# Attention stage of a fused layer: a half's statistics and normalisation one slot earlier, and POOL's casts of the fourth slot behind its splits

## The chip, the cores and the metric

The kernel runs on one core of one Trainium2 chip. The metric is the device time of one execution in microseconds (us). Engines are named as the profile names them: PE (TensorE matmul), PEld (its weight loads), DVE (VectorE), ACT (ScalarE), POOL (GpSimd) and SP (SyncE, which here only issues DMAs).

## What is computed

The input x is (16, 1024, 256) in float32. Four residual stages follow each other: a linear recurrence over time (SSM), a small gated network (FFN), causal attention, and the FFN once more. Only attention is touched:

```python
x = x + attn(layernorm(x))
# attn: x_proj = x @ Wqkv + bqkv; q, k, v = x_proj split in three
#       each reshaped (not transposed) from (1024, 256) to (16 heads, 1024, 16)
#       softmax(causal(q @ k.T / 4)) @ v, back to (1024, 256), then @ Wproj + bproj
# layernorm: (x - mean) / sqrt(var + 1e-5) over the 256 channels, no weights
```

Because of the plain reshape, head h is made of tokens 64h to 64h+63. A sequence of 1024 tokens so splits into two independent **halves** of 512 tokens and 8 heads each, and each half into two **quads** of 4 heads.

## The kernel before, in words

`attention_phase` (L1148) handles batch element b (0 to 15) in four **slots** q = 0 to 3, written here as the first, second, third and fourth slot. Slot q does quad 4b+q, and each slot has 20 **steps** (STEPS). The program is a loop nest unrolled in Python: every engine has a function `slot(b, q)` that collects tasks with a due step (a number, whole or not) and sorts them by it (`in_order`, L1308). The number only sets the order of an engine's own queue. An engine runs its queue strictly in that order and waits at semaphores where it must.

What runs in a slot:

- **Second pass** (all 20 steps). PE forms scores of the slot's quad with the row maxima as an extra row of the operands (L1878), ACT exponentiates them (L1738), and PE multiplies by v (L1906). Three PSUM banks, `s2_ps`, go round.
- **First pass** (steps 0 to 13 for the next quad, units 4 to 17; steps 16 to 19 for the quad after that, units 0 to 3). PE forms the plain scores (L1856), two products a step (one for each group of rows), DVE takes their row maxima (L1637, L1640) in `maxima`. Three banks, `s1_ps`, go round, so PE may start product n only when DVE has finished the maxima of product n-3 (`first_wait`, L1840). DVE's maxima of steps 4 and 13 end with a reduction and a 32x32 transpose, whose result SP moves by DMA (`move_max`, L1354).
- **x events** (`x_events`, L1187): the work that shares the single bank `x_ps`. "heads", "turn" and "out" finish earlier results. "project" with j = 0, 1 transposes the normalised x of a half, j = 2 to 5 gives q and k (L1934), and j = 6, 7 gives v. An event that stands at step n is issued by PE in step n+1. For the half 2b+3 the events j = 0, 1 are at steps 13, 15 of the second slot, and j = 2 to 7 at steps 3, 7, 9, 11, 13, 15 of the third. For the half 2b+4, j = 0 to 5 are at steps 3, 7, 9, 11, 13, 15 of the fourth, and j = 6, 7 at steps 3 and 7 of the next element's first slot.
- **Splits**. ACT copies the result of a project event with j < 6 to one of three buffers `full` (L1748, L1750), and POOL's `split` (L1468) writes it as two float32r parts: a cast (L1478) and a subtraction (L1480). PE's project j = 2 waits for the splits of both j = 0 and j = 1 (L1927).
- **Casts**. `lay_out` (L1482) casts the q and k stacks of quad+3 from `staged`, which SP's `load_stack` (L1331) has filled with 12 DMAs, into `qs` and `ks` (L1492). Per slot there are two sides and two pieces of each side. A small POOL instruction (L1490) goes ahead of each side and takes its waits. PE first reads these stacks at step 16 of the next slot. SP's next `load_stack` waits for them (L1336).
- **Statistics and normalisation** of a half of x. SP loads x (`load_x`, L1317), DVE's `prepare` (L1598) computes mean and variance (four L1604, a memset at L1610, four L1612), and POOL's `rstds` (L1449) and `normalise` (L1455) compute the reciprocal deviation (L1451, L1453) and normalise in place in four pieces (L1458). PE's project j = 0 waits for this (`xn_ready`). The statistics' tile `moments` is single, so `prepare` waits at L1608 for the previous half's normalisation.

The due steps of this work are constants:

```python
LAY_OUT_AT, PREPARE_AT, PIECES = (6.3, 7.6, 10.2, 12.2), 6, 2
NORMALISE_AT = (14.4, 15.5, 16.5, 17.5)
```

A half is prepared in the first slot (half 2b+3) and in the third slot (half 2b+4). SP loads the x of half 2b+4 in the first slot of the same b (due step 4, L1387).

Of the kernel before, what the change touches and what calls it, by code (L numbers as in the profile page):

```python
# [1147 lines left out]
def attention_phase(nc, sem, identf, identb, x2, x3, wqkv, bqkv, wproj, bproj, qk_scratch, v_scratch):  # L1148
# [25 lines left out]
    STEPS = 2 * UNITS2  # L1174
    LEAD = 4
    EVACUATE_AT = (7, 1)
    LAY_OUT_AT, PREPARE_AT, PIECES = (6.3, 7.6, 10.2, 12.2), 6, 2
    NORMALISE_AT = (14.4, 15.5, 16.5, 17.5)

    X_PROLOGUE = 22  # L1180
    FULLS = 3
# [5 lines left out]
    def x_events(q, first, more, more2):  # L1187

        heads = [] if first and q == 0 else [(1, "heads", 0), (7 if q == 1 else 5, "heads", 1)]
        finish = [] if first else {0: [(9, "turn", 0), (11, "out", 0), (13, "turn", 1), (15, "out", 1)],  # L1190
                                   1: [(3, "turn", 2), (5, "turn", 3), (9, "out", 2), (11, "out", 3)]}.get(q, [])
        project = {0: [(3, 6), (7, 7)], 1: [(13, 0), (15, 1)], 2: [(3, 2), (7, 3), (9, 4), (11, 5), (13, 6), (15, 7)],
                   3: [(3, 0), (7, 1), (9, 2), (11, 3), (13, 4), (15, 5)]}[q] if (more2 if q == 3 else more) else []
        return sorted(heads + finish + [(s, "project", j) for s, j in project])

    def flags(b):
        if isinstance(b, int):
            return b == 0, b + 1 < NB, b + 2 < NB
        return False, True, True
# [4 lines left out]
    def x_base(b, q):  # L1204

        before = X_PROLOGUE + sum(x_count(i) for i in range(b)) if isinstance(b, int) else \
            x_count(None) * b + (X_PROLOGUE + x_count(0) - x_count(None))
        return before + sum(len(x_events(i, *flags(b))) for i in range(q))

    def projected(b, q):  # L1210

        return ((2 * b + 2, 0), (2 * b + 3, 1), (2 * b + 3, 1), (2 * b + 4, 0))[q]
# [9 lines left out]
    with ExitStack() as ctx:  # L1222
# [85 lines left out]
        def in_order(tasks):  # L1308

            for _, task in sorted(tasks, key=lambda x: x[0]):  # L1310
                task()

        with nc.Block() as block:
# [129 lines left out]
            def _(pool):  # L1443
# [5 lines left out]
                def rstds(hb):  # L1449
                    pool.wait_ge(moments_done, hb + 1)  # L1450
                    g.tensor_tensor(var_eps[:, :], moments[:, :, 1], eps[:, :], ALU.add).then_inc(eps_added, 1)  # L1451
                    pool.wait_ge(eps_added, hb + 1)
                    g.tensor_tensor(rstd[:, :], var_eps[:, :], minus_half[:, :], ALU.pow).then_inc(rstd_ready, 1)  # L1453

                def normalise(hb, s, t):  # L1455
                    if t == 0:
                        pool.wait_ge(rstd_ready, hb + 1)
                    last = g.tensor_scalar(xt[s][:, t, :], xt[s][:, t, :], moments[:, t, 0:1], rstd[:, t:t + 1],  # L1458
                                           ALU.subtract, ALU.mult)
                    if t == TT - 1:  # L1460
                        last.then_inc(xn_ready, 1)
# [6 lines left out]
                def split(hb, j, index):  # L1468

                    n = 6 * (hb - 3) + j  # L1470
                    k = n % len(full)
                    pool.wait_ge(x_free, index + 1 - X_PROLOGUE)
                    if j < KT:
                        high, low = xnT[0][:, j, :], xnT[1][:, j, :]
                    else:
                        high, low = parts[:, j - KT, 0, :], parts[:, j - KT, 1, :]
                        pool.wait_ge(side_stored[(j - KT) // 2], 32 * hb)
                    g.tensor_copy(high, full[k][:, :]).then_inc(rounded, 1)  # L1478
                    pool.wait_ge(rounded, n + 1)
                    g.tensor_tensor(low, full[k][:, :], high.bitcast(F32), ALU.subtract).then_inc(split_done, 1)  # L1480
# [56 lines left out]
                def v_bias(hb, e, index):  # L1537
                    if index < X_PROLOGUE:
                        pool.wait_ge(v_free, 2 * hb + e + 1)
                    else:  # L1540
                        pool.wait_ge(x_free, index + 1 - X_PROLOGUE)
                    g.tensor_tensor(v_tok[:, 2 * e:2 * e + 2, :], v_tok[:, 2 * e:2 * e + 2, :],
                                    bv_row[:, :].unsqueeze(1).to_broadcast([P, 2, D]), ALU.add).then_inc(v_ready, 1)

                def bias(b, r):
                    pool.wait_ge(res_loaded[r % 2], 32 * b + 16 * (r // 2 + 1))
                    g.tensor_tensor(x_res[r % 2][:, :, :], x_res[r % 2][:, :, :],  # L1547
                                    bp_row[:, :].unsqueeze(1).to_broadcast([P, 2, D]), ALU.add).then_inc(bias_added, 1)

                def slot(b, q):  # L1550
                    first, more, more2 = flags(b)
                    quad = 4 * b + q
                    tasks = []
                    for n, (at, kind, which) in enumerate(x_events(q, first, more, more2)):
                        if kind == "project" and which >= 6:
                            tasks += [(at + 3, lambda e=which - 6, n=n: v_bias(projected(b, q)[0], e, x_base(b, q) + n))]
                        elif kind == "project":
                            tasks += [(at + 2, lambda j=which, n=n: split(projected(b, q)[0], j, x_base(b, q) + n))]
                    if q < 2 and not first:
                        tasks += [(4, lambda r=r: bias(b - 1, r)) for r in (2 * q, 2 * q + 1)]  # L1560
                    if q in (0, 2) and (more, None, more2)[q]:
                        hb, s = ((2 * b + 3, 1), None, (2 * b + 4, 0))[q]
                        tasks += [(NORMALISE_AT[0], lambda: rstds(hb))]
                        tasks += [(NORMALISE_AT[t], lambda t=t: normalise(hb, s, t)) for t in range(TT)]
                    if more or q == 0:
                        for side in range(2):
                            for e in range(PIECES):
                                tasks += [(LAY_OUT_AT[PIECES * side + e],
                                           lambda side=side, e=e: lay_out(quad + 3, side, e, not first or q > 0))]
                    in_order(tasks)  # L1570

                def sequence(b):
                    for q in range(4):
                        slot(b, q)
# [20 lines left out]
            def _(dve):  # L1595
                v = nc.vector

                def prepare(hb, s, turn):  # L1598
                    if not isinstance(hb, int) or hb > 0:

                        dve.wait_ge(moments_done, hb)
                    dve.wait_ge(x_loaded[s], 16 * turn + 16)
                    for t in range(TT):
                        last = v.bn_stats(stats[:, t, :], xt[s][:, t, :])  # L1604
                    last.then_inc(stats_done, 1)
                    if not isinstance(hb, int) or hb > 0:

                        dve.wait_ge(xn_ready, hb)  # L1608
                    dve.wait_ge(stats_done, hb + 1)
                    v.memset(carrier[:, :], 0.0)  # L1610
                    for t in range(TT):
                        last = v.bn_aggr(moments[:, t, :], stats[:, t, :])  # L1612
                    last.then_inc(moments_done, 1)
# [56 lines left out]
                def slot(b, q):  # L1670
                    first, more, more2 = flags(b)
                    tasks = []
                    for step in range(STEPS):
                        unit = first_pass_at(q, step, more)
                        if unit is not None:
                            tasks += [(step, lambda unit=unit: maxima(4 * b + q + unit[0], unit[1]))]
                    for n, (at, kind, which) in enumerate(x_events(q, first, more, more2)):
                        if kind == "heads":
                            before = (q - 1) % 4
                            tasks += [(at + 1, lambda e=which, n=n: divide(4 * b + q - 1, before, e, x_base(b, q) + n))]  # L1680
                        elif kind == "out":
                            tasks += [(at + 1, lambda r=which, n=n: add(b - 1, r, x_base(b, q) + n))]
                    if q in (0, 2) and (more, None, more2)[q]:
                        tasks += [(PREPARE_AT, lambda: prepare(*((2 * b + 3, 1, b + 1), None, (2 * b + 4, 0, b + 2))[q]))]
                    in_order(tasks)

                def sequence(b):
# [387 lines left out]
```

## Time and profile before

| | |
|---|---|
| three timed runs | 4064.49, 4067.5 (median), 4070.07 us |
| the profiled execution's own time | 4071.99 us |
| its span in the profile | 4070.2 us, 78382 instructions |
| busy over the span | PE 3703.5 us (91%), DVE 2935.1 (72%), ACT 2248.6 (55%), POOL 1702.0 (42%) |
| mean granted TensorE clock | 0.966 of full |

All rows are of this one profiled execution. "Busy" is the time in which an engine had an instruction in execution; the ends of matmuls are modelled. Stage and slot borders below are the starts of ACT's first exponential (L1738) of a slot. In a timeline row the first number is the start in us from the span's start, the second the length, and the bracket, where there is one, the engine's idle time ahead of it and what ended it. Rows of several instructions ("x4") run from the first's start to the last's end.

### The profile page before, as it was taken

The page shows a single profiled execution, that of the slowest core. Times are in us where ns is not written, and L with a number is a line of the kernel's source. Part 1 is how long each engine was busy: PE and PEld are TensorE (multiplying, and loading weights), DVE is VectorE, ACT ScalarE, POOL GpSimd, SP SyncE. Part 2 cuts the span into 40 slices and gives each one's busy share as a digit, 9 for nine tenths or more (in the row PEclk, how much of TensorE's full clock was granted, in tenths as well). Part 3 has the DMA queues.
Part 4 walks back from the last instruction along what each step waited for, and adds up shares of the span by engine and source line. Part 5 has one row for each costly group of instructions (what it writes and reads, how often), then busy time and mean ns, then how long its engine had stood idle before and what let it go on. Part 6 is the DMA issues. An engine that isn't in the chain of part 4 may idle for free. (4 is left out here: it accounts for less than half of the span.)

```text
span 4070.2 us, 78382 instructions
## 1 busy us (share of the span) xinstructions
PE 3703.5 (91%) x26254; PEld 2383.8 (59%) x26254; DVE 2935.1 (72%) x9262; ACT 2248.6 (55%) x4454; POOL 1702.0 (42%) x2042
## 2 busy tenths in 40 slices
PE   4998799999479999999999999999999996999997
PEld 4887566666245555555555555555555553666674
DVE  6997466756467877887787778778877882466675
ACT  0100356665136666666666666666666663566664
POOL 2332024232625555555464555556455510142422
PEclk9999799999669999999999999999999997999999
DMA  1332111111566778677777767787777731021111
GB/s 54 98 103 91 55 47 63 63 45 39 108 113 101 117 103 127 103 115 121 115 115 106 123 112 114 107 121 111 112 124 109 112 43 58 32 63 63 60 45 42
DMA packets 701473, 361.36 MB, mean 89 GB/s; under 512 B 305072, under 2 KB 668080, under 8 KB 701104
## 3 DMA queue, kind: packets, MB, share of 16 engines
q1 hardware_dynamic: 701104, 356.65, 48.9%
q8 instruction: 206, 3.38, 0.4%
q14 instruction: 163, 1.34, 0.2%
HBM read 204.49 MB, written 150.99 MB: 87 GB/s over the span
## 5 line engine op out<-in xcount | busy, mean ns | idle before, releaser
L1738 ACT ACTIVATE att_probs<-att_s 128x512 f32<-128x512 f32 (+1 forms) x2560 | 1319.1, 557 | 754.5 <-PE att_s L1826 429.4
L1637 DVE CUSTOM_DVE_ANT_0 att_s<-att_s,att_above 128x384 f32<-128x384 f32 (+3 forms) x2048 | 957.4, 514 | 190.6 <-PE att_s L1856 190.5
L1878 PE MATMUL att_s<-att_qs,att_ks 49*128 49x512 f32 (+3 forms) x3072 | 916.6, 387 | 101.6 <-ACT att_probs L1738 29.0
L1856 PE MATMUL att_s<-att_ks,att_qs 48*128 48x512 f32 (+3 forms) x3072 | 961.2, 407 | 23.6 <-POOL att_ks L1492 13.5
L1640 DVE TENSOR_REDUCE att_maxima<-att_s 128x1 f32<-128x512 f32 x1024 | 668.4, 682 | 248.6 <-PE att_s L1856 243.3
L1878 PEld LDWEIGHTS att_s<-att_qs,att_ks 49*128 49x128 f32 x3072 | 459.5, 185 | 661.4 <-ACT att_probs L1738 435.9
L1906 PE MATMUL att_o_ps<-att_probs,att_vs 128*32 128x512 f32 (+3 forms) x6144 | 630.2, 497 | 0.5 <-ACT att_probs L1738 0.5
L1856 PEld LDWEIGHTS att_s<-att_ks,att_qs 48*128 48x128 f32 x3072 | 486.1, 188 | 41.1 <-issue 16.9
L1057 PE MATMUL ffn_h2p<-ffn_h,ffn_w 128*128 128x512 f32 x768 | 365.6, 599 | 3.0 <-ACT ffn_h L938 0.9
L1826 PE MATMUL att_s<-att_mask,att_places 64*128 64x64 bf16 (+1 forms) x3072 | 332.7, 205 | 0.0
L1547 POOL TENSOR_TENSOR att_x_res<-att_x_res,att_bp_row 128x512 f32<-128x512 f32 x64 | 81.3, 1283 | 527.6 <-DMA att_x_res<-x 527.1
L916 ACT ACTIVATE ffn_uv<-ffn_uvp 128x512 f32<-128x512 f32 x256 | 153.3, 599 | 251.4 <-PE ffn_uvp L1032 251.4
L1637 DVE DVE_READ_ACCUMULATOR2_ANT att_maxima<- 128x1 f32 x2048 | 288.6, 141 | 0.0
L1492 POOL CAST att_ks<-att_staged 113x1024 fp32r<-113x1024 f32 x128 | 253.5, 1993 | 0.0
L946 ACT ACTIVATE ffn_h<-ffn_turned,ffn_b 128x512 f32<-128x512 f32 x384 | 242.6, 684 | 17.4 <-PE ffn_turned L1048 15.5
L1492 POOL CAST att_qs<-att_staged 113x1024 fp32r<-113x1024 f32 x128 | 251.9, 1991 | 0.0
L938 ACT ACTIVATE ffn_h<-ffn_h2p,ffn_b 128x512 f32<-128x512 f32 x192 | 132.0, 687 | 198.2 <-PE ffn_h2p L1057 198.2
L1906 PEld LDWEIGHTS att_o_ps<-att_probs,att_vs 128*32 128x32 f32 x6144 | 134.1, 108 | 161.1 <-issue 121.6
L675 POOL TENSOR_TENSOR ffn_var_eps<-ffn_moments,ffn_eps 128x4 f32<-128x4 f32 x64 | 13.1, 204 | 500.8 <-DVE ffn_moments L760 500.8
L775 DVE TENSOR_TENSOR ffn_zT_lo<-ffn_zTp,ffn_zT_hi 128x512 fp32r<-128x512 f32 x128 | 87.8, 686 | 182.3 <-ACT ffn_zT_hi L908 182.3
L1934 PE MATMUL att_x_ps<-att_xnT,att_wqkv 128*128 128x512 f32 x714 | 200.7, 417 | 19.9 <-POOL att_xnT L1480 19.7
L1048 PEld LDWEIGHTS ffn_turned<-identf,ffn_uv 128*128 128x128 f32 x1536 | 175.5, 143 | 64.6 <-issue 43.5
(247 smaller groups left out, 6559.9 us busy)
## 6 DMA issues: line engine op xcount, KB each, us to landing
att_staged<-qk_scratch SPq DMA_DIRECT2D x768, 128.0 KB, 7.1
qk_scratch<-att_parts SPq DMA_DIRECT2D x128, 512.0 KB, 3.7
ffn_x<-x SPq DMA_DIRECT2D x64, 512.0 KB, 5.0
ssm_x<-in_L_attn_a_x_dram SPq DMA_DIRECT2D x32, 512.0 KB, 3.8
x<-ssm_y SPq DMA_DIRECT2D x32, 512.0 KB, 2.9
x<-ffn_y SPq DMA_DIRECT2D x32, 512.0 KB, 2.9
att_x<-x SPq DMA_DIRECT2D x32, 512.0 KB, 11.9
v_scratch<-att_v_tok SPq DMA_DIRECT2D x32, 512.0 KB, 3.5
```

What stands on the lines that cost most here:

```text
L946: last = a(h1[k][:, f, :], turned_ps[:, f, :], ACT.Gelu, bias=b1[:, f:f + 1])
L1048: last = pe.transpose(turned_ps[:, f, t * P:(t + 1) * P], of[:, t, f * P:(f + 1) * P], identf[:, :])
L1057: last = mm(h2_ps[:, :], w2[:, f, :], h1[k][:, f, :], start=(f == 0), stop=(f == KT - 1))
L1492: last = g.tensor_copy(stack[0:ROWS, :].rearrange("p (t c) -> p t c", c=HD)[:, e * n:(e + 1) * n, :], staged[side][0:ROWS, :, e * n:(e + 1 ...
L1637: last = v.tensor_tensor_reduce(scores, scores, above[:, CH - w:CH], 1.0, -3.0e38, ALU.add, ALU.max, to)
L1640: last = v.tensor_reduce(to, scores, AX.X, ALU.max)
L1738: a(probs[u % 2][2 * g + p][:, 0:n], bank[:, 0:n], ACT.Exp).then_inc(exp_done, 1)
L1826: last = mm(blocks[:, at, GROUP * half:GROUP * (half + 1)], places[rows, 2 * (1 - k) + half, :], mask[rows, 1 - k, 0:len(cols), :], start= ...
L1856: last = mm(bank[:, col:col + w], rows_of(qs[buf], g, KROWS, p, BT * blk, BT * (blk + 1)), rows_of(ks[buf], g, KROWS, p, t0, t1), start=k ...
L1878: last = mm(bank[:, col:col + w], rows_of(ks[buf], g, SHIFT + 1, p, BT * j, BT * (j + 1)), rows_of(qs[buf], g, SHIFT + 1, p, t0, t1), star ...
L1906: last = mm(o_ps[32 * i:32 * i + 32, HD * (t0 - first_t):HD * (t1 - first_t)], vs[s][:, NBLK * head + j, :], probs[u % 2][i][:, col:col + ...
L1934: last = mm(bank[:, :], wq[i][:, f, cols], xnT[k][:, f, :], start=(n == 0), stop=(n == KT * len(PARTS_R) - 1))
```

## The change

The first slot and the third slot prepared a half each. Now it is the first and the second: the half 2b+4 is measured by DVE (due step 6) and normalised by POOL (due steps 13.2, 14.7, 16.7, 18.7) in the second slot. The same due steps for POOL now hold in the first slot, too. In the fourth slot alone POOL's four casts get the due steps 10.2, 12.2, 14.2, 16.2, so that they stand behind the splits of j = 0 and 1 (due 5 and 9) and between those of j = 2 to 5 (due 11, 13, 15, 17). PE's, ACT's and SP's orders are untouched, and no instruction is added or taken away.

```diff
-    LAY_OUT_AT, PREPARE_AT, PIECES = (6.3, 7.6, 10.2, 12.2), 6, 2
-    NORMALISE_AT = (14.4, 15.5, 16.5, 17.5)
+    LAY_OUT_AT = [(6.3, 7.6, 10.2, 12.2)] * 3 + [(10.2, 12.2, 14.2, 16.2)]
+    PREPARE_AT, PIECES = 6, 2
+    NORMALISE_AT = (13.2, 14.7, 16.7, 18.7)
...
-                    if q in (0, 2) and (more, None, more2)[q]:
-                        hb, s = ((2 * b + 3, 1), None, (2 * b + 4, 0))[q]
+                    if q < 2 and (more, more2)[q]:
+                        hb, s = ((2 * b + 3, 1), (2 * b + 4, 0))[q]
                         tasks += [(NORMALISE_AT[0], lambda: rstds(hb))]
                         tasks += [(NORMALISE_AT[t], lambda t=t: normalise(hb, s, t)) for t in range(TT)]
...
-                                tasks += [(LAY_OUT_AT[PIECES * side + e],
+                                tasks += [(LAY_OUT_AT[q][PIECES * side + e],
...
-                    if q in (0, 2) and (more, None, more2)[q]:
-                        tasks += [(PREPARE_AT, lambda: prepare(*((2 * b + 3, 1, b + 1), None, (2 * b + 4, 0, b + 2))[q]))]
+                    if q < 2 and (more, more2)[q]:
+                        tasks += [(PREPARE_AT, lambda: prepare(*((2 * b + 3, 1, b + 1), (2 * b + 4, 0, b + 2))[q]))]
```

The half 2b+4 exists for b = 0 to 13 (`more2`), so both moves touch 14 elements.

## Rows read from the trace of the kernel before

**Rows 1.** Stretch, length; PE, PEld, DVE, ACT, POOL busy (instructions); PE's clock, DMA share, GB/s.

```profile
1170.90:3394.30 2223.40, 2114.30 (x18162) 1227.77 (x18161) 1751.74 (x5849) 1486.54 (x2981) 1150.50 (x1010) 0.99 0.72 108
```

**Rows 2.** PE's waits in the attention stage: total us, times, longest us.

```profile
PE att_s L1878 <- DVE att_maxima L1640: 28.6, 41, 1.5
PE att_x_ps L1934 <- POOL att_xnT L1480: 19.7, 14, 2.4
```

**Rows 3.** Busy time by stretch: the four slots of element 3.

```profile
1599.09:1634.03 34.94, 33.90 (x299) 20.48 (x298) 28.84 (x96) 22.88 (x47) 18.88 (x16) 1.00 0.93 131
1634.03:1666.28 32.25, 31.53 (x283) 18.18 (x282) 27.52 (x91) 22.68 (x47) 14.65 (x13) 1.00 0.60 83
1666.28:1703.03 36.75, 35.11 (x299) 20.86 (x298) 28.43 (x98) 24.24 (x49) 24.18 (x22) 1.00 0.80 126
1703.03:1738.76 35.73, 33.44 (x283) 18.75 (x283) 27.16 (x92) 24.08 (x49) 19.47 (x18) 1.00 0.64 116
```

**Rows 4.** Timeline of element 3's fourth slot, ACT, POOL and PE.

```profile
1716.21 0.61 ACT L1748 ACTIVATE att_full<-att_x_ps 128x512 f32<-128x512 f32 x1
...
1717.58 1.27 POOL L1480 TENSOR_TENSOR att_xnT<-att_full,att_xnT 128x512 fp32r<-128x512 f32 x1
...
1719.00 0.47 PE L1934 MATMUL att_x_ps<-att_xnT,att_wqkv 128*128 128x512 f32 x1 [1.01 <-POOL att_xnT L1480]
```

**Rows 5.** The same place of element 9: POOL's timeline, then PE's.

```profile
2554.09 0.18 POOL L1490 TENSOR_TENSOR att_pool_carrier<-att_eps 1x1 f32<-1x1 f32 x1 [1.13 <-DMA att_staged<-qk_scratch]
...
2560.22 0.70 PE L1934 MATMUL att_x_ps<-att_xnT,att_wqkv 128*128 128x512 f32 x2 [2.13 <-POOL att_xnT L1480]
```

**Rows 6.** Busy time by stretch: fourth slots of elements 0 to 13, two and the sum.

```profile
1420.88:1459.45 38.57, 34.91 (x283) 19.39 (x281) 27.16 (x92) 24.07 (x48) 19.40 (x18) 0.96 0.64 107
...
2543.13:2579.96 36.83, 33.43 (x283) 18.73 (x283) 27.15 (x92) 24.07 (x49) 19.44 (x18) 1.00 0.67 113
...
sum 509.89, PE 472.43 PEld 264.73 DVE 380.27 ACT 337.17 POOL 272.56; mean PE 33.74 PEld 18.91 DVE 27.16 ACT 24.08 POOL 19.47
```

**Rows 7.** Busy time by stretch: third slots of elements 13 and 14.

```profile
3069.64:3106.39 36.75, 35.11 (x299) 20.85 (x298) 28.44 (x98) 24.24 (x48) 24.20 (x22) 1.00 0.79 127
...
3209.28:3244.83 35.55, 34.83 (x299) 20.76 (x298) 26.87 (x89) 24.24 (x49) 18.22 (x16) 1.00 0.87 129
```

**Rows 8.** Timeline of element 13's third slot, DVE and PE.

```profile
3081.87 1.39 DVE L1604 BATCH_NORM_STATS2 att_stats<-att_x 128x6 f32<-128x256 f32 x4
...
3083.70 1.25 DVE L1640 TENSOR_REDUCE att_maxima<-att_s 128x1 f32<-128x512 f32 x2
...
3085.10 0.49 PE L1856 MATMUL att_s<-att_ks,att_qs 48*128 48x512 f32 x1
```

**Rows 9.** DVE's timeline in element 3's second slot, steps 7 to 11.

```profile
1644.77 1.28 DVE L1640 TENSOR_REDUCE att_maxima<-att_s 128x1 f32<-128x512 f32 x2
...
1647.75 0.42 DVE L1659 TENSOR_TENSOR att_y<-att_x_ps,att_recip 128x256 f32<-128x256 f32 x1
...
1650.97 0.43 DVE L1637 CUSTOM_DVE_ANT_0 att_s<-att_s,att_above 128x256 f32<-128x256 f32 x1 [0.82 <-PE att_s L1856]
```

**Rows 10.** PE's timeline there, steps 9 and 10.

```profile
1646.42 0.40 PE L1856 MATMUL att_s<-att_ks,att_qs 48*128 48x512 f32 x1
...
1648.46 0.48 PE L1963 MATMUL att_x_ps<-att_wproj,att_yT 128*128 128x256 f32 x1
```

**Rows 11.** POOL's timeline: end of element 3's first slot, then its second slot.

```profile
1629.37 4.84 POOL L1458 TENSOR_SCALAR att_x<-att_x,att_moments,att_rstd 128x256 f32<-128x256 f32 x4
...
1659.50 0.62 POOL L1478 CAST att_xnT<-att_full 128x512 fp32r<-128x512 f32 x1 [6.42 <-ACT att_full L1748]
1662.46 0.61 POOL L1478 CAST att_xnT<-att_full 128x512 fp32r<-128x512 f32 x1 [0.98 <-ACT att_full L1748]
```

**Rows 12.** The load of x in element 3's first slot (line 1317), and its time to landing.

```profile
L1317 SPq DMA_DIRECT2D att_x<-x x1: 11021/11021/11021, 1607.5 to 1607.5; - x1
...
DMA to landing us min/median/max: 15.8/15.8/15.8
```

## The prediction, made before the changed kernel was run

> **What bounds the kernel now.** I read the busy times by stretch first. The attention stage takes 2223.4 us of the span, and PE is busy for 2114.3 of them [rows 1], so PE sets the pace and a step saves time only where PE stands still or is held. Second, PE's waits in that stage: two kinds matter here. PE waits 19.7 us in 14 places for POOL's split of the transposed x, and 28.6 us in 41 places for DVE's row maxima [rows 2]. Third, the slots of one undisturbed element: 34.94, 32.25, 36.75 and 35.73 us, with DVE busy 28.84, 27.52, 28.43 and 27.16 us [rows 3]. The reader is to see that the second slot is the shortest, so that DVE has the least room there: 4.7 us of it are free, against 8.3 in the third.
>
> **The casts in the fourth slot.** The 14 waits for POOL are one in each fourth slot of elements 0 to 13: project j = 2 needs the split of j = 1, due 9, and two casts stand ahead of that (due 6.3 and 7.6). How much are the casts to blame? In element 3 ACT's copy ends at 1716.21 + 0.61 = 1716.82; POOL's subtraction starts at 1717.58, which leaves place for nothing but the split's own cast of 0.6; it ends at 1718.85, and PE starts at 1719.00 after standing still for 1.01 us [rows 4]. So POOL was free just as the copy came, and **1.01 us of the wait are the length of copy and split**, which the change doesn't touch. In element 9 it is different: POOL's small instruction ahead of the casts waited 1.13 us for the stack's DMA, all behind it came 1.1 us later, and PE stood still for 2.13 us [rows 5]. That excess goes, because the casts no longer stand ahead. It is 19.7 - 14 x 1.01 = 5.6 us in all [rows 2, 4].
>
> The slots' lengths show a second part. The 14 fourth slots take 509.89 us; 14 of 35.73 would be 500.22, so the excess is 9.7 us, 5.6 of it the waits [rows 3, 6]. The rest is in three slots whose granted clock is 0.96 (one is shown, 38.57 us): the clock was at 1.2 GHz instead of 2.4 for a short time behind a stall of 1.9 to 2.4 us, and that costs (9.7 - 5.6) / 3 = 1.4 us each. Element 9, with 2.13 us, kept 1.00 [rows 6]. With stalls of 1.0 us I expect no fall. The sum by this: -5.6 - 4.1 = **-9.7 us** against the profiled execution. (The Trainium skill, "TensorE: Matmul & The Clock Gate", section "Why this matters for your kernels", ties a drop in mid-kernel to idle gaps longer than any here; by it these stalls didn't cause the falls, and the second term would be 0. The rows speak for the stalls, as all three falls lie in slots with a long one.)
>
> Behind the splits the casts have room. From step 10 on a split (0.61 + 1.28) and a cast (2.0) come to 3.9 us, and project events come every two steps, some 4.0 us apart in that slot. It fits with almost nothing over; the last split may slip by 0.1 us, and with it SP's last store and the next slot's stack loads. PE reads those stacks only at step 16 of the next slot. Cost 0; if the fit fails, SP is late with the next `load_stack`, the residual's load and POOL's bias behind it.
>
> **The statistics leave the third slot.** Element 14 has no such half, so its third slot shows what remains: 35.55 us against 36.75, and DVE 26.87 busy instead of 28.44 [rows 7]. The saving is 1.20 us a slot, 14 x 1.20 = **-16.8 us**. The mechanism: from the statistics' start at 3081.87 to the maxima behind them at 3083.70 DVE is taken for 1.83 us; the maxima end at 3084.95, and PE's next product that needs their bank starts at 3085.10, 0.15 us later [rows 8]. So 0.15 us is the hand-over when PE is held. What DVE's 1.83 us cost PE is 1.83 less the slack over 0.15 that PE has there. POOL's four normalisations leave this slot too; nobody on PE's path waits for them.
>
> **They enter the second slot.** DVE's same 1.83 us now come after the maxima of step 6, ahead of those at 1644.77. These end at 1646.05, and PE's product starts at 1646.42: a slack of 0.37, or 0.22 over the hand-over [rows 9, 10]. PE is delayed 1.83 - 0.22 = 1.61 us. DVE has no idle time there until 1650.97, where it is 0.82 us [rows 9], so nothing ahead absorbs it. The division behind those maxima also comes 1.83 us later: it ends at 1648.17, and PE's event that needs the bank starts at 1648.46 [rows 9, 10], 0.29 of which 0.14 is slack, so that the delay could be 1.69. Bounds: from above the whole 1.83; from below 1.20, what the third slot paid with more slack. I take 1.65, nearer the rows of this slot: 14 x 1.65 = **+23.1 us**. So the move of DVE's work loses 6.3 us: it costs more where DVE has less room.
>
> What else enters there: POOL's two small operations and four normalisations, 4.84 us for four [rows 11]. POOL is idle 6.42 us ahead of the split of j = 0 and 0.98 ahead of j = 1 [rows 11]. Two of the normalisations fit into the first; the third makes the split of j = 1 late by about 0.2 us, but its reader on PE is in step 4 of the third slot, over 5 us away. The fourth is behind. Cost 0; without that cover PE would wait for the split at 1.2 us a normalisation. `prepare` gains two waits in DVE's queue, with all maxima behind them. The x: issued at 1607.5 it has landed 15.8 us later, at 1623.3, before the second slot starts at 1634.03 [rows 3, 12]. The first slot's normalisation ends at 1629.37 + 4.84 = 1634.21 [rows 11], some 12 us ahead of DVE's aggregation. In the first slot the new due steps change nothing, since no other POOL task has a due step over 12.2. PE's first reader of the half is in the fourth slot, a whole slot later. SP gets the third slot's last store a little sooner, as POOL's v bias no longer stands behind normalisations; the stack's DMAs of the fourth slot start earlier, which helps the casts a second time.
>
> **The sum.** Against the profiled execution's 4072.0: -9.7 - 16.8 + 23.1 = -3.4, 4068.6 us. The median of the timed runs, 4067.5, is 4.5 us lower. Late DMAs and falls of the clock differ from run to run, and this profile may have had more than most. If the whole 4.5 is of that kind, the median gives 4067.5 + 6.3 - 5.2 = 4068.6; if none, 4067.5 + 6.3 - 9.7 = 4064.1. I take **4067 us**, no change that can be told. About 0.2%, 8 us, is what a measurement of this kernel can tell.
>
> **The rivals.**
> - *Faster: DVE catches up in the second slot.* PE's spacing there may itself hold small waits for DVE that give way once PE is late. Then the cost may fall to half the third slot's, 0.6 us: 14 x (0.6 - 1.2) - 5 to -10 = about -15, 4053 us. For it: PE's busy time holds modelled ends. Against it: DVE is without idle time up to 1650.97 [rows 9], so what was added must show. Chance 0.14.
> - *Slower: the clock falls in the second slot.* The place is steps 8 to 10, the price 1.4 us at each fall. It decides from the point where a stall there is long enough; 1.61 us lies between 1.01 and 1.9, where the rows show no fall and falls. In 10 of 14 slots this gives 4067 + 14 = 4081 us; in all, 4087. Against it: the stall comes in two pieces, as two products wait. Chance 0.14.
> - *The clock's falls don't hang on the stalls.* All three may have fallen in a fourth slot by chance. Then they remain, and with them up to 4.1 us: 4071 us. Chance 0.08, no sign. (The rule of the Trainium skill's page cited above would have it so.)
> - *The change misses its aim in the fourth slot:* POOL, now full from step 10 on, hands over splits and stacks late, and the lateness goes round by SP. Some 0.5 us in each of 14 slots, 4074 us. Chance 0.08.
>
> **How the numbers follow.** My forecast has the remaining 0.56, within 4060 to 4075: its lower end is the cost in the second slot at 1.2 us (-6.3), its upper end 1.83 (+2.5) and no gain from the rarer late DMAs (+5.2). The range for 8 in 10 reaches half-way to the two outer cases: 4057 to 4079. Faster by over 0.2% is below 4059.4: the first rival and a little of the forecast, 0.16. Slower is above 4075.6: the second, some of the last two and of the forecast, 0.20. Within: 0.64.
>
> **What would show it.** In the changed profile the second slots take about 33.9 us, with PE's waits for DVE's maxima at steps 8 and 9; the third slots 35.55; the fourth 35.7 in every element, with a wait of 0.95 to 1.0 us for the split and no other; the clock 1.00 throughout the slots. The first slot stays at 34.9. I am wrong if the second slot grows by less than 1.2 or more than 1.9 us, if its clock falls, if the fourth slot's wait goes below 0.9 us, or if PE waits for `xn_ready`.

## The result and the profile after

The changed kernel takes **4090.65 us** (median of 4 runs, 4087.82 to 4096.26) against 4066.9 for the kernel before; the ratio is 1.0061, 95% interval 1.0048 to 1.0075. It is slower by 0.6%, and the forecast of no change was wrong. The profiled execution took 4087.82 us with a span of 4086.0, where before it was 4071.99 and 4070.2. All line numbers from L1177 on are one higher than before.

The first view is the busy time by stretch for the second slots of elements 0 to 13 (stretch, length; PE, PEld, DVE, ACT, POOL busy; granted clock of PE; DMA share; GB/s). In [rows 3] the second slot was 32.25 us at clock 1.00.

```profile
1350.24:1386.00 35.76, 33.38 (x284) 19.36 (x282) 29.31 (x100) 22.88 (x46) 20.30 (x19) 0.95 0.53 74
1492.20:1529.09 36.89, 34.91 (x284) 19.68 (x282) 29.30 (x100) 22.89 (x46) 20.18 (x18) 0.91 0.57 73
1635.27:1672.29 37.02, 34.96 (x284) 19.81 (x282) 29.30 (x100) 22.89 (x46) 20.33 (x18) 0.91 0.46 72
1778.47:1813.89 35.42, 33.36 (x283) 18.61 (x282) 29.29 (x100) 22.89 (x46) 20.85 (x19) 0.95 0.56 76
1920.07:1953.96 33.89, 31.82 (x284) 18.24 (x282) 29.21 (x100) 22.89 (x47) 20.35 (x18) 1.00 0.46 77
...
sum 497.23, PE 467.33 PEld 264.71 DVE 408.58 ACT 319.56 POOL 285.60; mean PE 33.38 PEld 18.91 DVE 29.18 ACT 22.83 POOL 20.40
```

The reader is to see two things. Element 5 (the last single row) has clock 1.00 and takes 33.89 us, so DVE's work costs 33.89 - 32.25 = 1.64 us. In 11 of the 14 slots the clock was below 1.00, and among elements 1 to 13 such a slot is longer again by 1.5 to 1.6 us (0.95) or 3.0 to 3.2 us (0.91); element 1's 1.9 us hold 0.3 us of a longer wait. I call such a stretch at the lower level a fall of the clock. The clock has only the levels 1.2 and 2.4 GHz here, so 0.95 of 35.42 us is some 3.5 us at the lower level, and 0.91 of 37.02 some 6.7 us; in the trace a fall lasts 3.4 or 6.8 us here.

The same view of element 3's third and fourth slots, with the sums over elements 0 to 13:

```profile
1672.29:1707.84 35.55, 34.83 (x300) 20.76 (x298) 26.87 (x89) 24.22 (x48) 18.16 (x16) 1.00 0.86 128
...
sum 498.08, PE 487.89 PEld 290.80 DVE 376.20 ACT 339.16 POOL 254.87; mean PE 34.85 PEld 20.77 DVE 26.87 ACT 24.23 POOL 18.20
```

```profile
1707.84:1743.55 35.71, 33.43 (x283) 18.72 (x282) 27.18 (x92) 24.06 (x48) 19.48 (x18) 1.00 0.59 119
...
sum 500.01, PE 468.14 PEld 262.26 DVE 380.55 ACT 336.89 POOL 272.64; mean PE 33.44 PEld 18.73 DVE 27.18 ACT 24.06 POOL 19.47
```

Against the kernel before, whose sums were 449.86, 515.29 and 509.89 us for the second, third and fourth slots, this is +47.4, -17.2 and -9.9. The first slots became 2.4 us shorter, 2.0 of it in element 0, where the clock varied in both profiles. Of the +47.4 the longer stall makes 14 x 1.64 = 23.0. Fourteen second slots at their undisturbed length, with element 0 at 29.60 + 1.64, would come to 471.8; so the falls of the clock made 497.2 - 471.8 = **25.4 us**, with under 1 us in it for longer waits in elements 0 and 1 (1.5 and 1.6 us where the others have 1.25). The two come to 48.4, 1.0 more than 47.4, because the kernel before had a wait of 1.5 us at the start of element 10's second slot (33.34 us) that is missing here. In all, the attention stage takes 19.4 us longer (2242.8 against 2223.4 in [rows 1]), and the rest of the span came out 3.6 us shorter, which the change doesn't touch.

PE's waits in the attention stage (total, times, longest), where [rows 2] had 28.6 us for DVE in 41 places and 19.7 us with a longest of 2.4 for POOL:

```profile
PE att_s L1879 <- DVE att_maxima L1641: 32.8, 37, 1.6
...
PE att_x_ps L1935 <- POOL att_xnT L1481: 14.2, 14, 1.0
```

All fourteen waits for the split are now 1.0 us. Last, the place of the fall in element 3: DVE's timeline, then PE's, then the stretches about it.

```profile
1646.01 1.40 DVE L1605 BATCH_NORM_STATS2 att_stats<-att_x 128x6 f32<-128x256 f32 x4
...
1647.84 1.26 DVE L1641 TENSOR_REDUCE att_maxima<-att_s 128x1 f32<-128x512 f32 x2
```

```profile
1648.65 0.46 PE L1879 MATMUL att_s<-att_qs,att_ks 49*128 49x512 f32 x1 [1.25 <-DVE att_maxima L1641]
...
1649.25 0.76 PE L1879 MATMUL att_s<-att_qs,att_ks 49*128 49x512 f32 x1
1649.25 0.79 PE L1857 MATMUL att_s<-att_ks,att_qs 48*128 48x512 f32 x1
```

```profile
1645.80:1649.20 3.40, 2.10 (x20) 1.26 (x12) 3.28 (x14) 2.54 (x7) 3.40 (x4) 1.00 0.42 46
1649.20:1652.60 3.40, 3.35 (x14) 1.18 (x15) 2.58 (x11) 1.15 (x2) 3.40 (x2) 0.50 0.01 1
1652.60:1656.00 3.40, 3.40 (x12) 2.64 (x9) 1.47 (x5) 1.08 (x2) 3.21 (x5) 0.50 0.00 0
1656.00:1659.40 3.40, 3.40 (x23) 1.67 (x23) 2.42 (x7) 1.88 (x4) 0.43 (x1) 0.99 0.01 5
```

DVE is taken by the statistics from 1646.01 to 1647.84, 1.83 us as before the move. PE stands still for 1.25 us, does one round, is held again for 0.1 us (the second maxima end at 1649.10, its product starts at 1649.25), and just then the clock drops to 0.50. A product of 512 columns that took 0.40 us [rows 10] takes 0.79. PE is "busy" throughout the low stretch, with 12 to 14 matmuls in 3.4 us instead of 23, so this loss is in no list of waits. It shows in the clock column and in the slots' lengths alone.

### The profile page after: what moved, and what is told of

Same layout as the page of the kernel before. It is cut to its first block and busy times, and to the rows that moved or that the text cites. A ratio compares the mean times of both kernels' runs of the same rounds, so it can differ in the third digit from the quotient of the medians.

```text
span 4086.0 us, 78382 instructions
## 1 busy us (share of the span) xinstructions
PE 3719.9 (91%) x26254; PEld 2390.4 (59%) x26254; DVE 2938.4 (72%) x9262; ACT 2250.0 (55%) x4454; POOL 1699.4 (42%) x2042
## 3 DMA queue, kind: packets, MB, share of 16 engines
q1 hardware_dynamic: 701104, 356.65, 48.4%
## 5 line engine op out<-in xcount | busy, mean ns | idle before, releaser
L1879 PE MATMUL att_s<-att_qs,att_ks 49*128 49x512 f32 (+3 forms) x3072 | 923.3, 390 | 107.3 <-DVE att_maxima L1641 32.8
L1641 DVE TENSOR_REDUCE att_maxima<-att_s 128x1 f32<-128x512 f32 x1024 | 669.5, 682 | 261.1 <-PE att_s L1857 256.1
L1048 PE MATMUL ffn_turned<-identf,ffn_uv 128*128 128x128 f32 x1536 | 202.9, 275 | 9.5 <-DVE ffn_uv L800 7.4
```

Of the source, the lines that this page charges most:

```text
L1048: last = pe.transpose(turned_ps[:, f, t * P:(t + 1) * P], of[:, t, f * P:(f + 1) * P], identf[:, :])
L1641: last = v.tensor_reduce(to, scores, AX.X, ALU.max)
L1879: last = mm(bank[:, col:col + w], rows_of(ks[buf], g, SHIFT + 1, p, BT * j, BT * (j + 1)), rows_of(qs[buf], g, SHIFT + 1, p, t0, t1), star ...
```

## The experiments

The theory: the loss is the second slot's stall for DVE, and the clock falls behind it. The rivals: that the casts' new places cost, that POOL's normalisation in the second slot does, or that the falls belong to something other than the stall.

**1. The casts alone.**

```diff
--- before
-    LAY_OUT_AT, PREPARE_AT, PIECES = (6.3, 7.6, 10.2, 12.2), 6, 2
+    LAY_OUT_AT = [(6.3, 7.6, 10.2, 12.2)] * 3 + [(10.2, 12.2, 14.2, 16.2)]
+    PREPARE_AT, PIECES = 6, 2
...
-                                tasks += [(LAY_OUT_AT[PIECES * side + e],
+                                tasks += [(LAY_OUT_AT[q][PIECES * side + e],
```

> The kernel before with the new due steps of the fourth slot's casts alone. Stall theory (the loss is the second slot's stall for DVE and the falls of PE's clock behind it): the second slots stay at 32.25 us at clock 1.00, the third at 36.75, the fourth come to 35.72 in all of elements 0 to 13; 4057 to 4064 us. Rival (the casts behind the splits are what costs): 4075 us or more, with fourth slots above 36.

Measured: 4058.24 us against 4066.66, ratio 0.9986 (0.9974 to 0.9997). Its fourth slots, one and the sum:

```profile
1697.43:1733.14 35.71, 33.42 (x283) 18.74 (x283) 27.15 (x92) 24.08 (x49) 19.52 (x18) 1.00 0.60 116
...
sum 500.60, PE 468.54 PEld 262.52 DVE 380.18 ACT 337.13 POOL 273.15; mean PE 33.47 PEld 18.75 DVE 27.16 ACT 24.08 POOL 19.51
```

This half of the change is a small gain: 509.89 - 500.60 = 9.3 us in these profiles. It doesn't need the other half. The rival falls.

**2. The statistics of the second slot at step 14**, behind the row maxima.

```diff
--- after
-    PREPARE_AT, PIECES = 6, 2
+    PREPARE_AT, PIECES = (6, 14), 2
...
-                        tasks += [(PREPARE_AT, lambda: prepare(*((2 * b + 3, 1, b + 1), (2 * b + 4, 0, b + 2))[q]))]
+                        tasks += [(PREPARE_AT[q], lambda: prepare(*((2 * b + 3, 1, b + 1), (2 * b + 4, 0, b + 2))[q]))]
```

> The changed kernel with DVE's statistics of the second slot due at step 14, where no row maxima stand, instead of 6. Stall theory: DVE's work then costs PE nothing; second slots 32.25 to 32.6 us without a fall of the clock, third 35.55, fourth 35.72; 4040 to 4050 us. Rival (what loses time is that POOL normalises in the second slot, or that the x is read there): second slots stay at 34 us or more, 4080 to 4092 us.

Measured: 4046.23 us, ratio 0.9947 (0.9929 to 0.9964). Second slots of elements 3 and 10:

```profile
1627.94:1660.18 32.24, 31.53 (x283) 18.18 (x282) 29.08 (x100) 22.67 (x46) 16.46 (x16) 1.00 0.59 83
...
2598.64:2642.30 43.66, 41.85 (x283) 23.01 (x282) 30.02 (x100) 23.14 (x46) 18.52 (x18) 0.73 0.50 73
```

DVE is as busy as in the changed kernel, 29.08 us, and POOL still normalises here, but apart from elements 2 (32.51) and 10 the slots are as long as before, 32.25 us, and 29.60 in element 0. So neither POOL's work nor the reading of x costs PE time. It is the place in DVE's queue. Element 10's slot is an exception, for a reason of its own. PE stood still for 1.49 us at the slot's start, a wait that the kernel before has in that place, too (1.5 us, and a slot of 33.34), and behind it the clock stayed low:

```profile
2600.39 0.54 PE L1879 MATMUL att_s<-att_qs,att_ks 49*128 49x512 f32 x1 [1.49 <-DVE att_maxima L1641]
```

```profile
2605.00:2612.00 7.00, 7.00 (x45) 3.84 (x45) 4.24 (x15) 2.71 (x6) 2.12 (x2) 0.50 1.20 161
2612.00:2620.00 8.00, 8.00 (x47) 4.14 (x39) 4.83 (x15) 4.10 (x10) 6.21 (x6) 0.50 0.68 59
```

The trace has the clock at 0.50 for 23.9 us here, while PE was busy all the time. Against the same slot with the same wait and no fall, 33.34 us, this one fall cost 10.3 us (43.66 - 33.34). The profiled execution, 4056.08 us, was the slowest of its four.

**3. POOL's normalisation back in the third slot**, DVE's statistics left in the second.

```diff
--- after (in POOL's slot alone)
-                    if q < 2 and (more, more2)[q]:
-                        hb, s = ((2 * b + 3, 1), (2 * b + 4, 0))[q]
+                    if q in (0, 2) and (more, None, more2)[q]:
+                        hb, s = ((2 * b + 3, 1), None, (2 * b + 4, 0))[q]
```

> The changed kernel with POOL's normalisation back in the third slot, DVE's statistics left in the second at step 6. Stall theory: as the changed kernel, second slots 33.9 us with clock 1.00 and 35.4 to 37 us in most elements, where the clock falls; 4087 to 4096 us. Rival (POOL's normalisation in the second slot is the cause): second slots 32.25, 4065 us or less.

Measured: 4081.43 us, ratio 1.0031 (1.0016 to 1.0046). Undisturbed second slots take 33.87 or 33.88 us (element 1's 34.19), as with POOL's work there, and the clock falls in 6 of 14. So POOL's place isn't the cause. But 6 falls are not 11, and the time is under what I expected, which run 8 takes up.

**4. The kernel before, with more work for DVE.** Nothing is moved; five statistics instructions with a result that nobody reads go to step 6 of the second slot.

```diff
--- before
+        unread = sb("unread", [P, 5, 6])
...
+                    if q == 1 and more2:
+                        tasks += [(PREPARE_AT, lambda t=t: v.bn_stats(unread[:, t, :], wp[:, t % 2, :])) for t in range(5)]
```

> The kernel before with five more statistics instructions (some 1.75 us of DVE, result unread) at step 6 of the second slot of elements 0 to 13; nothing else moved. Stall theory: second slots at least 33.8 us, and falls of the clock there in some 8 to 13 of the 14 elements, at 1.5 or 3.1 us each; 4105 to 4115 us. Rival (the falls need the moved work elsewhere, an emptier third or fourth slot): second slots 33.8 us at clock 1.00, 4089 us.

Measured: 4103.43 us, ratio 1.0097 (1.0061 to 1.0132). Second slots of elements 2 to 4:

```profile
1493.87:1530.74 36.87, 34.98 (x283) 19.80 (x282) 29.23 (x96) 22.91 (x46) 14.32 (x12) 0.91 0.53 71
1638.31:1672.01 33.70, 31.80 (x284) 18.25 (x282) 29.14 (x96) 22.89 (x46) 14.63 (x13) 1.00 0.53 79
1779.98:1815.24 35.26, 33.37 (x283) 18.89 (x282) 29.23 (x96) 22.90 (x47) 15.88 (x14) 0.95 0.58 80
```

The stall alone, without the change, brings the 1.45 us and the falls (6 of 14), behind waits of 1.1 us. I had expected 8 to 13 falls and 4105 to 4115 us, a little too many. With runs 2 and 3 this isolates the cause.

**5. The statistics at step 10** (run 2's edit, with 10 for 14).

> The changed kernel with DVE's statistics of the second slot due at step 10 instead of 6. By the slack rule (cost to PE = 1.83 us less the slack over 0.15 us of the product that reads the bank of the maxima behind): the slack there is 1.45, so 1.83 - 1.30 = 0.5 us; second slots 32.8 us. Stall theory: no fall of the clock there, about 4050 us. Rival (the second slot's clock falls because the statistics are in it, wherever): falls in several elements, 4070 us or more.

Measured: 4056.04 us, ratio 0.9974 (0.9959 to 0.9988), 6 us above what I expected. The second slots of elements 1 to 13 all take 32.78 to 32.81 us, at clock 1.00:

```profile
1632.54:1665.34 32.80, 31.87 (x283) 18.34 (x282) 29.08 (x100) 22.79 (x47) 20.46 (x19) 1.00 0.61 81
```

The slack rule said 32.8. Only element 0's slot shows a fall, behind a wait of 1.7 us, and it lies some 5 to 7 us later in the slot than those of the changed kernel.

The profiled execution took 4069.0 us, the slowest of its eight, and its trace shows where that went. In element 15, the last, the clock fell behind a wait of 0.66 us and stood at 0.50 for 37.6 us; its third and fourth slots took 37.83 and 30.70 us, where the kernel before had 28.86 and 25.73.

```profile
3336.48 0.47 PE L1879 MATMUL att_s<-att_qs,att_ks 49*128 49x512 f32 x1 [0.66 <-DVE att_maxima L1641]
```

```profile
3340.00:3374.00 34.00, 33.35 (x188) 15.45 (x187) 7.50 (x27) 16.46 (x34) 2.50 (x2) 0.50 0.06 17
```

So a wait of over a microsecond isn't needed everywhere: in the last two elements, whose slots have less work in them, falls came behind 0.7 us in seven of the eleven profiles.

**6. The statistics at step 14 in the first slot, too.** In the second slot POOL's normalisation also moves, behind the two splits.

```diff
--- after, with run 2's edit
-    PREPARE_AT, PIECES = (6, 14), 2
-    NORMALISE_AT = (13.2, 14.7, 16.7, 18.7)
+    PREPARE_AT, PIECES = (14, 14), 2
+    NORMALISE_AT = ((13.2, 14.7, 16.7, 18.7), (17.1, 17.2, 17.3, 17.4))
...
-                        tasks += [(NORMALISE_AT[0], lambda: rstds(hb))]
-                        tasks += [(NORMALISE_AT[t], lambda t=t: normalise(hb, s, t)) for t in range(TT)]
+                        tasks += [(NORMALISE_AT[q][0], lambda: rstds(hb))]
+                        tasks += [(NORMALISE_AT[q][t], lambda t=t: normalise(hb, s, t)) for t in range(TT)]
```

> The changed kernel with DVE's statistics due at step 14 in the first slot, too, and POOL's normalisation of the second slot behind its two splits. Stall theory: first slots lose the 1.04 us that PE waits for row maxima, 33.7 to 33.9 us; second 32.25, third 35.55, fourth 35.72; no fall of the clock; 4025 to 4032 us, the fastest of all. Rival (PE's first slot is held by something else behind the maxima): first slots 34.9, 4040 us or more.

Measured: **4027.78 us**, ratio 0.991 (0.9888 to 0.9931), the fastest of all and ahead of both kernels. A first slot, and PE's wait for the row maxima:

```profile
1588.20:1621.92 33.72, 33.59 (x299) 20.43 (x298) 28.84 (x96) 22.86 (x46) 17.51 (x15) 1.00 0.93 129
```

```profile
PE att_s L1879 <- DVE att_maxima L1641: 5.4, 12, 1.4
```

The first slot paid 1.2 us for the same mistake of place, 34.94 against 33.72. PE's total wait behind L1641 went from the changed kernel's 32.8 us to 5.4. My expectation of no fall holds among the slots of elements 1 to 13 but for element 10, whose second slot took 37.69 us at clock 0.86, behind a wait of 1.4 us at its start.

**7. A shorter stall** (run 4 with `range(3)` for `range(5)`).

> The kernel before with three more statistics instructions (some 1.1 us of DVE) at step 6 of the second slot, where five gave 33.70 us. By the slack rule 0.8 us a slot: second slots 33.05 us at clock 1.00, +11 us. Stall theory with a length that decides: no or few falls of the clock, 4078 to 4083 us. Rival (any added DVE work there brings the falls): half of the elements at 34.5 us or more, 4095 us.

Measured: 4080.16 us, ratio 1.0027 (1.0015 to 1.0039), and none of the 14 second slots has a fall. PE stands still there for 0.44 us in one piece, where run 4 has 1.09:

```profile
1635.00:1668.05 33.05, 31.80 (x283) 18.25 (x282) 28.48 (x94) 22.89 (x46) 15.25 (x13) 1.00 0.61 83
```

**8. The changed kernel again.** No edit.

> The changed kernel once more, on the chip of these runs. If the number of falls of the clock hangs on chance from run to run, the profile shows another number than 11 of 14 and other elements, and the time lies between 4078 and 4096 us. If it is fixed by the program, 11 again, 4087 to 4096 us, while the kernel with POOL's normalisation in the third slot keeps its 6.

Measured: 4081.14 us (4073.71 to 4106.03, 9 runs), ratio 1.0034 (1.0013 to 1.0055). Six of 14 second slots show a lower clock (elements 0 to 4 and 6), where the first profile had 11. Element 3's and the sum:

```profile
1635.85:1672.80 36.95, 34.88 (x284) 19.74 (x282) 29.28 (x100) 22.89 (x46) 20.30 (x18) 0.91 0.45 70
...
sum 484.21, PE 453.63 PEld 258.15 DVE 408.29 ACT 319.67 POOL 289.89; mean PE 32.40 PEld 18.44 DVE 29.16 ACT 22.83 POOL 20.71
```

The undisturbed ones are again 33.87 to 33.90 us but for element 9's 34.15. So the 1.64 us are the program's. The number of falls is not: it differs between two profiles of one program. It isn't all chance either, since elements 0 to 4 and 6 fell in both, elements 1 to 4 with the same clocks. The profiled execution took 4087.19 us in spite of its fewer falls there, partly since element 15's first slot fell, too (38.47 us at clock 0.82, against 32.31). The loss of the change, by the medians of the two comparisons, lies between some 12 and 24 us. Run 3 with its 6 falls and 4081 us is the same as this, no gain.

**9. A stall of the same length in another slot.** Run 2's kernel, and seven unread statistics instructions at step 6 of the third slot.

```diff
--- after, with run 2's edit
+        unread = sb("unread", [P, 7, 6])
...
+                    if q == 2 and more2:
+                        tasks += [(6, lambda t=t: v.bn_stats(unread[:, t, :], wp[:, t % 2, :])) for t in range(7)]
```

> The kernel with the second slot's statistics at step 14, and seven unread statistics instructions (some 2.4 us of DVE) at step 6 of the third slot of elements 0 to 13, so that PE meets a stall as long as the changed kernel's, in another slot. Slack rule: 2.4 less 0.63 of slack is 1.8 us; third slots 37.3 us. If the stall's length decides alone: falls of the clock in a good part of the third slots (38.8 or 40.4 us), 4080 us or more. If the second slot's own pattern of work is needed, too (it has transposes and small products about step 8, the third has a projection): third slots 37.3 us at clock 1.00, 4070 us.

Measured: 4067.55 us (9 runs), ratio 1.001 (0.9999 to 1.0021) to the kernel before. Third slots of elements 1 and 3:

```profile
1382.52:1421.30 38.78, 36.66 (x299) 21.42 (x298) 29.02 (x96) 24.24 (x49) 22.42 (x20) 0.96 0.80 130
...
1664.35:1701.57 37.22, 35.09 (x299) 20.85 (x298) 29.04 (x96) 24.24 (x49) 22.46 (x20) 1.00 0.86 136
```

```profile
1679.69 0.46 PE L1882 MATMUL att_s<-att_qs,att_ks 49*128 49x512 f32 x1 [1.32 <-DVE att_maxima L1642]
```

The slot grew to 37.22 us where the slack rule said 37.3, and PE's stall is 1.32 us, as long as the changed kernel's. The clock fell in 3 of 14. So neither answer came out clean: a stall of this length can bring a fall in another slot, too, but here it did so more seldom than the 11 and 6 of the second slot. With one profile for this kernel and such variation between profiles, whether the slot's pattern of work matters is open.

## Why the prediction was wrong

- **The fourth slot: right.** "1.01 us of the wait are the length of copy and split" stands: 14.2 us in 14 places, longest 1.0, and 35.7 us in every element. The excess went, 9.9 us of a forecast 9.7, and run 1 gives it alone. That POOL's casts and splits just fit is borne out as well: POOL runs on from one to the other and the fourth slot doesn't lengthen. That the falls there went with the long waits holds in every profile: with the casts in their new place (the changed kernel twice and runs 1, 2, 3, 5, 6 and 9) none of 8 x 14 fourth slots fell, and with the old place (the kernel before, runs 4 and 7) 5 of 3 x 14 did, each behind a wait of 1.8 to 2.4 us.
- **The third slot: right.** 35.55 us against 35.55, and 17.2 us in all for 16.8.
- **The second slot's stall: right.** 1.64 us against 1.65. The rule behind it, DVE's added time less the slack of the product that reads the bank, over a hand-over of 0.15 us, gave 32.8 and 33.05 us in two other runs, which measured 32.80 and 33.05.
- **Nothing from POOL, SP or the load of x: right**, by runs 2 and 3.
- **The step that failed: the term for the second slot, "14 x 1.65 = +23.1 us", which put the falls of the clock there at nothing.** The stall in it was right, but the second slots grew by 47.4 us, because the clock fell in 11 of 14 and that made 25.4 us. The prediction had this as its second rival, at 0.14. It set the chance low for two reasons. By its rows there was no fall at 1.01 us and there were falls only from 1.9 us on; that left 1.61 in between, and I counted the gap as mostly safe with nothing to say so. The trace of the kernel before even had a counterexample where I didn't look: in element 14's fourth slot the clock fell to 0.50 behind a wait of 0.67 us (the two rows below). And "the stall comes in two pieces" was taken as a protection; it came as 1.25 and 0.1 us, and the fall in element 3 came right behind the second piece.

```profile
3257.02 0.46 PE L1878 MATMUL att_s<-att_qs,att_ks 49*128 49x512 f32 x1 [0.67 <-DVE att_maxima L1640]
```

```profile
3258.20:3261.60 3.40, 3.34 (x18) 1.35 (x11) 2.26 (x8) 1.46 (x3) 2.14 (x2) 0.50 0.01 1
```

- **The price of a fall was sized too low.** I had 1.4 us from three falls at 0.96, and the short ones cost 1.5 to 1.6. But six of the 11 falls lasted twice as long, and the five of them in elements 2 to 13 cost 3.0 to 3.2 us, so that the rival's own time, 4081 for 10 falls and 4087 for all, was still under the measured 4090.65 of the first comparison. That the repetition's median, 4081.14, is the rival's 4081 is luck: its one profile had six falls in the second slots and took 4087.19.
- **The rule of the Trainium skill** ("TensorE: Matmul & The Clock Gate", section "Why this matters for your kernels"), which ties a drop in mid-kernel to idle gaps longer than these, is no safe bound here: the longest wait for the row maxima is 1.6 us, and the clock fell in up to 11 of 14 second slots. Removing the stall removed the falls but for one behind another wait (run 2), and adding it to the kernel before brought them (run 4). The rival built on the rule is out as well: no fourth slot of elements 0 to 13 in the changed kernel had a fall.

The failure was thus not in the sum of busy and idle times, which came out within 0.5 us a part, but in a cost that no wait shows.

## What to carry to other kernels

Before work is moved in an engine's queue, read the slack of what stands behind it at the new place: the same 1.83 us of DVE cost PE 1.64 us at step 6 of the second slot, 0.55 at step 10 and nothing at step 14. And where a change makes PE wait in a new place, look at the clock by stretch: here waits of 1.1 to 1.6 us brought falls in 3 to 11 of 14 slots, and those of the first profile doubled the price of the stall (25.4 us on 23.0), while 0.44 us (run 7) brought none. These are no thresholds, as falls behind 0.7 us in the last elements show. A change with two parts is to be timed by its parts; one of these was a gain of 0.14% and hid behind the other.

## What the runs showed of the hardware

- PE's clock fell behind waits of 1.1 to 1.6 us in one piece with 0.1 us shortly behind (second slots of the changed kernel, of runs 3 and 4, third slots of run 9), and not once in 14 second slots behind the 0.44 us of run 7, nor in the first slots of elements 1 to 13 of the kernel before (0.8 us in element 3's). The same wait brought a fall in some elements and none in others: in the changed kernel's elements 3 and 5 it is 1.3 us in both, and only element 3's clock fell. In the stretch ahead of element 3's fall PE was busy for 2.10 of 3.40 us. What decides is open.
- In the last two elements 0.67 us was enough (the kernel before, element 14, shown above; run 5, element 15).
- A fall costs about 1.5 us when it lasts 3.4 us and 3.1 us when it lasts 6.8; both occurred in one execution, at the same place in the slot.
- The same program showed 11 falls in one profile and 6 in another, and its timed runs spread from 4073.71 to 4106.03 us, where those of the kernel before in that comparison spread from 4060.67 to 4078.87.
- A fall can also last much longer: in run 2 one held the clock at 0.50 for 23.9 us with PE busy throughout and cost 10.3 us, behind a single wait of 1.49 us.
- The profile puts that wait, at the start of element 10's second slot (in the kernel before and in runs 2 and 6), down to DVE's row maxima, but DVE is not late there: in run 2 its maxima start 0.4 us behind the slot's start, as in element 9 (2599.01 in a slot from 2598.64, 2460.58 in one from 2460.20). What is late is SP, which issues the DMAs of the row maxima that PE's queue waits for at step 1 (L1360, `max_moved`). Element 10's, then element 9's:

```profile
2593.77 5.52 SPq L1360 DMA_DIRECT2D att_qs<-att_row_max_T  x8
2599.33 0.44 SPq L1371 DMA_DIRECT2D x<-att_x_res  x1
```

```profile
2451.90 5.69 SPq L1360 DMA_DIRECT2D att_qs<-att_row_max_T  x8
```

  The eight end 0.65 us behind the slot's start in element 10 and 2.6 us ahead of it in element 9; in the kernel before it is 0.6 behind and 2.7 ahead. When they landed isn't in the trace, so this is argued and not shown; why SP is late in that element stays open.
